# Counts as logarithms in the exponent of a gathered attention: fused add and maximum in place of mask and count products, on one Trainium2 core

## The reference, cut to what matters

```
q = (x_q @ W_q.T).reshape(b, nq, H, HD)
c_sel = c_kv[jnp.arange(b)[:, None, None], indices]
kv = (c_sel @ W_kv_up.T).reshape(b, nq, K, 2, H, HD)
scores = jnp.einsum('bqhd,bqkhd->bqkh', q, k) * SCALE
attn = jax.nn.softmax(scores, axis=2)
out = jnp.einsum('bqkh,bqkhd->bqhd', attn, v).reshape(b, nq, d)
return out @ W_out.T
```

## Time and profile before

| | us |
|---|---|
| median of 3 runs | 1254.29 (1249.91 to 1254.9) |
| the profiled execution | 1254.05 |
| its span | 1252.6 |
| PE busy | 1171.6 (94%) |
| DVE busy | 980.0 (78%) |
| ACT busy | 913.4 (73%) |
| POOL busy | 640.3 (51%) |
| granted PE clock, mean | 0.975 of full |

### The profile page before, as it was taken

How to read it: one execution, slowest core, us unless ns; L and a number is a source line. 1 busy time by engine, 2 the same in 40 slices (tenths; PEclk the granted TensorE clock), 3 DMA queues, 4 the chain that set the end, 5 groups by cost and what they waited for, 6 DMA issues and landing times.

```text
span 1252.6 us, 30881 instructions
## 1 busy us (share of the span) xinstructions
PE 1171.6 (94%) x12256; PEld 952.0 (76%) x12256; DVE 980.0 (78%) x2026; ACT 913.4 (73%) x2290; POOL 640.3 (51%) x632
## 2 busy tenths in 40 slices
PE   2668999999999999999999999999999999999986
PEld 1446878788887777888888788888887888878864
DVE  3655888888888888888888888888888888877642
ACT  2365778778777877777778778777787787777751
POOL 2413455655544655554456555544565555445553
PEclk7877999999999999999999999999999999999998
DMA  8233112222221222122212221222222212212111
GB/s 285 69 72 98 49 49 59 49 55 72 59 56 41 58 53 54 37 53 64 83 45 58 49 55 40 53 59 51 83 58 49 59 38 52 59 39 52 30 25 23
DMA packets 82246, 74.82 MB, mean 60 GB/s; under 512 B 33017, under 2 KB 66239, under 8 KB 82102
## 3 DMA queue, kind: packets, MB, share of 16 engines
q1 hardware_dynamic: 81670, 71.89, 22.6%
q10 hardware_dynamic: 432, 0.95, 0.2%
HBM read 39.98 MB, written 15.52 MB: 44 GB/s over the span
## 4 chain that ended last, share of the span: by engine, by line
PE 85%; DMA 5%; SPq 3%; ACT 3%; DVE 2%; POOL 1%; issue 1%; ACTq 0%; POOLq 0%; DVEq 0%
PE F L391 15%; PE F L737 5%; PE TA L684 5%; PE F L385 5%; PE F L789 5%; PE F L764 5%; PE F L725 5%; PE F L800 4%; PE F L655 3%; PE SA L673 3%; PE SA L678 3%; PE F L794 3%; PE MA L691 3%; PE F L960 3%; PE TA L385 2%; PE F L781 2%
## 5 line engine op out<-in xcount | busy, mean ns | idle before, releaser
L1334 POOL TENSOR_TENSOR ZREST<-HID,ZPARTS 128x128 f32<-128x128 f32 x32 | 13.8, 431 | 218.9 <-ACT ZPARTS L1205 218.9
L1365 POOL TENSOR_TENSOR LS<-LS,ZABS 128x1024 f32<-128x1024 f32 x32 | 75.5, 2359 | 58.0 <-ACT ZABS L1278 58.0
L673 PE MATMUL SA<-MASK,minus 128*128 128x308 bf16 x256 | 73.0, 298 | 22.0 <-DMA QS<-q_dram 20.7
L665 DVE TENSOR_REDUCE PACKED<-HOT 128x19 int32<-128x1216 bf16 x64 | 92.2, 1441 | 0.1
L1321 POOL CAST IW<-IDX 128x64 f32<-128x64 int32 x32 | 8.0, 250 | 160.9 <-DMA IDX<-idx_dram 160.9
L684 PE MATMUL TA<-CONST,EXPS 128*128 128x128 f32 x512 | 87.6, 294 | 0.8 <-ACT OT L1270 0.8
L1355 POOL TENSOR_TENSOR QM<-QD,ISEXPT 128x1024 f32<-128x1024 f32 x32 | 75.9, 2372 | 5.0 <-DMA QD<-QG 4.9
L684 PEld LDWEIGHTS TA<-CONST,EXPS 128*128 128x128 f32 x512 | 72.0, 209 | 6.5 <-issue 5.1
L1357 POOL TENSOR_TENSOR AT<-AT 128x1024 f32<-128x1024 f32 x32 | 75.9, 2371 | 0.8 <-DVE AT L1055 0.8
L1358 POOL TENSOR_TENSOR QM<-QD,ISEXPT 128x1024 f32<-128x1024 f32 x32 | 76.0, 2375 | 0.0
L678 PE MATMUL SA<-KNOW,QS 128*128 128x154 bf16 x512 | 73.1, 232 | 0.0
(11 more groups left out here) (269 smaller groups left out, 3958.7 us busy)
## 6 DMA issues: line engine op xcount, KB each, us to landing
QD<-QG SPq DMA_DIRECT2D x128, 128.0 KB, 2.4
QS<-q_dram SPq DMA_DIRECT2D x64, 192.0 KB, 3.2
q_dram<-QPARTS SPq DMA_DIRECT2D x32, 192.0 KB, 2.1
XA<-x_dram SPq DMA_DIRECT2D x32, 128.0 KB, 2.2
QS<-q_dram SPq DMA_DIRECT2D x32, 128.0 KB, 2.4
XB<-x_dram SPq DMA_DIRECT2D x32, 128.0 KB, 3.0
out_dram<-OUT SPq DMA_DIRECT2D x32, 128.0 KB, 1.7
KNOW<-k_dram SPq DMA_DIRECT2D x4, 616.0 KB, 4.6
```

The costliest lines, as they stand in the source:

```text
L665: return dve.tensor_reduce(PACKED[:, r], HOT[:, r, :], AX.X, ALU.add)
L673: pe.matmul(SA[:, i, 0:2 * NKV], minus[:, :], MASK[t % 2][:, :].unsqueeze(1).to_broadcast([P, 2, NKV]), start=True, stop=False, skip_group ...
```

## The change

Counts enter before the exponential, as `LNC` = ln(count + 1e-30), with -1e30 added where the count is under 0.5. ACT makes the logarithm, POOL the rest, once a tile:

```diff
-                act.activation(COUNTR[:, :, :], COUNT[:, P:NPAD].unsqueeze(2).to_broadcast([P, RPAD, GH]), ACT.Copy).then_inc(s_a_counts_act, 1)
-                act.activation(COUNTT[a % 2][:, :, :], spares, ACT.Copy).then_inc(s_a_countt, 1)
-                act.activation(MASK[a % 2][:, :], COUNT[:, 0:NKV], ACT.Relu, bias=const("masked"), scale=MASKED).then_inc(s_a_counts_act, 1)
+                act.activation(LN[:, :], COUNT[:, 0:NKV], ACT.Ln, bias=const("tiny")).then_inc(s_a_lncount, 1)
...
+                pool.tensor_scalar(OFF[:, :], COUNT[:, 0:NKV], 0.5, MASKED, ALU.is_lt, ALU.mult).then_inc(s_a_off, 1)
+                pool.tensor_tensor(LNC[a % 2][:, :], LN[:, :], OFF[:, :], ALU.add).then_inc(s_a_counts_pool, 1)
```

The mask matmuls and the count transposes go. The maximum becomes one fused instruction for each head, which writes -(s + LNC) back to PSUM and keeps its minimum; the exponential then has scale -1:

```diff
-                pe.matmul(SA[:, i, 0:2 * NKV], minus[:, :], MASK[t % 2][:, :].unsqueeze(1).to_broadcast([P, 2, NKV]),
-                          start=True, stop=False, skip_group_check=True)
...
+        def maxima(t, out):
+            for h in range(GH):
+                s = score_banks[:, h // 2, h % 2, :]
+                last = dve.tensor_tensor_reduce(s, s, LNC[t % 2][:, :], -1.0, LARGE, ALU.add, ALU.min, out[:, h:h + 1])
+            return last
...
-                dve.tensor_reduce(MAXS[:, 0, :].rearrange("p (a h) -> p a h", a=2), score_banks, AX.X, ALU.max, negate=True).then_inc(s_b_max, 1)
+                maxima(b, MAXS[:, 0, :]).then_inc(s_b_max, 1)
...
-                act.activation(EXPS[:, 0, 0:NKV, 0], score_banks[:, 0, 0, :], ACT.Exp, bias=MAXS[:, 0, 0:1])
+                act.activation(EXPS[:, 0, 0:NKV, 0], score_banks[:, 0, 0, :], ACT.Exp, bias=MAXS[:, 0, 0:1], scale=-1.0)
```

`TA` and `MA` become neighbouring banks of one tile `TM`, so that the five transposed blocks of a group are 640 columns in a row (`ROWS`) and leave PSUM in one copy: on DVE for groups 0 and 2, on ACT for groups 1 and 3:

```diff
-                dve.tensor_tensor(PR[0][:, :], MA[:, 3 * P:4 * P], COUNTT[b % 2][:, 1, :], ALU.mult).then_inc(s_b_probr, 1)
-                dve.tensor_tensor(PT[0][:, :, :], TA[:, :].rearrange("p (h q) -> p h q", h=GH), COUNTT[b % 2][:, 0, :].unsqueeze(1).to_broadcast([P, GH, P]), ALU.mult).then_inc(s_b_probs, 1)
+                dve.tensor_copy(PT[0][:, :], ROWS).then_inc(s_b_probs, 1)
...
-                dve.tensor_tensor(PT[1][:, :, :], TA[:, :].rearrange("p (h q) -> p h q", h=GH), COUNTT[b % 2][:, 0, :].unsqueeze(1).to_broadcast([P, GH, P]), ALU.mult).then_inc(s_b_probs, 1)
-                dve.tensor_tensor(PR[1][:, :], MA[:, 3 * P:4 * P], COUNTT[b % 2][:, 1, :], ALU.mult).then_inc(s_b_probr, 1)
+                act.activation(PT[1][:, :], ROWS, ACT.Copy).then_inc(s_b_probs_act, 1)
```

More of the change, by code:

```diff
@@ L152, in program @@
         XNT = sb("XNT", [P, KD, P])
-        MASK = two("MASK", [P, NKV], bf16)
-        COUNTT = two("COUNTT", [P, 2, P])
+        LN = sb("LN", [P, NKV])
+        OFF = sb("OFF", [P, NKV])
+        LNC = two("LNC", [P, NKV])
         QT = sb("QT", [P, KD, P])
@@ L162, in program @@
         EXPS = sb("EXPS", [P, 2, NPAD, GH])
-        PT = two("PT", [P, GH, P])
-        PR = two("PR", [P, P])
+        PT = two("PT", [P, (GH + 1) * P])
         OT = sb("OT", [P, GROUPS, P])
@@ L694, in values @@
                 h = g * GH + hh
-                last = pe.matmul(o[VW * hh:VW * hh + VW, :], v[:, h * VW:(h + 1) * VW], PT[g % 2][:, hh, :],
+                last = pe.matmul(o[VW * hh:VW * hh + VW, :], v[:, h * VW:(h + 1) * VW], pt[:, cols(hh)],
                                  start=False, stop=True, skip_group_check=True)
@@ L839, in pe_tiles @@
                 transposes(C0, XM[:, :], KD).then_inc(s_c_xmt_ps, 1)
-            if 0 <= b < TILES:
-                scores(b, 1).then_inc(s_b_scores, 1)
+            if 0 <= d < TILES:
+                pe.wait_ge(s_d_k1, d + 1)
+                pairs(D2, lambda k, p: WQKB[:, cols(p)], lambda k: HQ[d % 2][:, :]).then_inc(s_d_q2_ps, 1)
             if 0 <= a < TILES:
@@ L852, in pe_tiles @@
             if 0 <= d < TILES:
-                pe.wait_ge(s_d_k1, d + 1)
-                pairs(D2, lambda k, p: WQKB[:, cols(p)], lambda k: HQ[d % 2][:, :]).then_inc(s_d_q2_ps, 1)
+                pe.wait_ge(s_d_exp2, 3 * d + 3)
+                transposes(D0, flat(K2[d % 2][:, :, :]), NP).then_inc(s_d_k2t_ps, 1)
             if 0 <= c < TILES:
@@ L861, in pe_tiles @@
                 hidden(XMT[c % 2]).then_inc(s_c_hidden_ps, 1)
[L862 to L866, removed]
             if 0 <= b < TILES:
-                pe.wait_ge(s_b_probs, 4 * b + 1)
-                values(b, 0).then_inc(s_b_values, 1)
+                pe.wait_ge(s_b_probs, 2 * b + 1)
+                values(b, 0, PT[0]).then_inc(s_b_values, 1)
+                pe.wait_ge(s_b_exps2_1, b + 1)
+                scores(b, 2).then_inc(s_b_scores, 1)
             if 0 <= c < TILES:
@@ L873, in pe_tiles @@
             if 0 <= d < TILES:
[L874 to L878, removed]
+                pe.wait_ge(s_d_q2, d + 1)
+                inner(KG1T, Q1).then_inc(s_d_a1_ps, 1)
             if 0 <= c < TILES:
@@ L883, in pe_tiles @@
                 pe.wait_ge(s_b_ot, 4 * b + 1)
-                exp_transposes(1).then_inc(s_b_exps_ps, 1)
+                exp_transposes(EXPS[:, 1]).then_inc(s_b_exps_ps, 1)
+            if 0 <= d < TILES:
+                pe.wait_ge(s_d_kg2, d + 1)
+                transposes(D0, flat(KG1T[:, :, :]), NP).then_inc(s_d_k1t_ps, 1)
+                pe.wait_ge(s_d_at1, d + 1)
+                inner(KG2T, QG2).then_inc(s_d_a2_ps, 1)
+            if 0 <= b < TILES:
+                pe.wait_ge(s_b_probs_act, 2 * b + 1)
+                values(b, 1, PT[1]).then_inc(s_b_values, 1)
+            if 0 <= c < TILES:
+                pe.wait_ge(s_c_zmin, 3 * c + 1)
+                v_product(XMT[c % 2]).then_inc(s_c_v_ps, 1)
             if 0 <= d < TILES:
@@ L1046, in dve_tiles @@
-                dve.tensor_tensor(PR[1][:, :], MA[:, 3 * P:4 * P], COUNTT[b % 2][:, 1, :], ALU.mult).then_inc(s_b_probr, 1)
+                dve.wait_ge(s_b_scores, 4 * b + 4)
+                maxima(b, MAXS[:, 1, :]).then_inc(s_b_max, 1)
+                dve.wait_ge(s_b_exps_ps, 4 * b + 3)
+                dve.tensor_copy(PT[0][:, :], ROWS).then_inc(s_b_probs, 1)
+            if 0 <= c < TILES:
+                dve.wait_ge(s_c_rexp, c + 1)
+                dve.tensor_reduce(RT[:, 2:3], ELOG[:, :], AX.X, ALU.add).then_inc(s_c_router, 1)
```

399 lines of the change are left out of this document (186 added, 213 removed).

## The result

The changed kernel takes 1259.36 us (median of 9 runs, 1256.86 to 1259.87) against 1252.35 for the kernel before (9 runs). The ratio is 1.0051, with a 95% interval of 1.0039 to 1.0063: about half a per cent slower, where 1232 us and 1.8% less were forecast. The profiled spans are 1258.6 and 1252.6 us.

The account below looks back on a forecast made before the run. PE was taken to bound the kernel, with DVE arriving last at the second `inner` after the change. Period 35.2 for 35.94 saves 21 us over 29 iterations, draining 1: 1254 - 22 = 1232 us, range 1212 to 1266.

Parts of the forecast that it names:

- PE, what goes: Mask matmuls leave PE, 1.05 us an iteration; PE reaches the second `inner` at T0 + 14.91, 19.71 remain; PE-only period 34.6.
- T0: Start on PE of the scores of group 0 in an iteration; times within the iteration count from it.
- DVE, what comes: DVE gets 16 fused pairs an iteration and two copies for four pairs; net only +0.2 us an iteration.
- t: DVE slot of one fused add-and-minimum pair, body plus read: taken as 0.30 us, bounds 0.25 to 0.46.
- 11.9 + 12 t: When DVE's `AT1` lets the second `inner` start, in us after T0; 15.5 with t = 0.30.
- The new wait: PE waits 0.6 us at the second `inner` for DVE's `AT1`, part of it earlier, at the transposes of `XN`.
- the rival at 1287 us: Fused body and read each wait for the other's end: t = 0.46, period 37.1, slower; chance 0.18.
- the forecast of 35.2: Steady period in us, 15.5 to the second `inner` plus 19.7 after it; 0.72 less than 35.94.
- ACT, POOL and SP at nothing, "0 to 0.5 us an iteration": Extra ACT and POOL work and unchanged SP DMAs cost nothing, being covered; 0 to 0.5 us kept for the range.
- The filling waits for the same DMAs.: The first iterations, before the steady period, wait for the same DMAs as before; no change in time counted.
- delays one ACT copy: POOL's `QREST`, behind another product of 2.37 us, delays an ACT copy ahead of `OT`'s second copy; costed at nothing.
- rival 2: Gain eaten: t 0.34 to 0.38, or 0.5 us of ACT-POOL waits; period 35.7 to 36.2, 1246 to 1260 us; chance 0.20.

## Why the prediction was wrong

- **PE, what goes.** Right: scores 0.27, rest of the iteration 19.70. PE's own arrival at the second `inner` was put at T0 + 14.91. With the exponential moved it is 15.22, of which 0.28 is the wait for `XN`: 14.94 without. Single distances changed both ways (`L707` 1.08 us for 0.90, the transposes of `K` 0.64 for 0.53, a wait of 0.21 for `XN` in the kernel before gone) and nearly cancel; why was not tried.
- **DVE, what comes.** t was 0.30 and is 0.27; the read costs no slot. The formula for `AT1`, 11.9 + 12 t, gives T0 + 15.1 with this t; in the kernel with the exponential moved it is ready at 14.91 (268.90 + 0.06 - 254.05). The rule of the Trainium skill that the next instruction waits for an empty pipeline, and with it the rival at 1287 us, did not come true; the section itself adds that an instruction that is not held starts earlier, and the starts 0.07 to 0.08 before the end of the one ahead agree with that.
- **The new wait.** Half right. PE does wait for a later DVE, but not at `inner`, in neither kernel: the wait is at `XN`, where the prediction put a part of it, 0.28 in place of 0.6. Nor does it hang on t: `KG1T`, moved ahead of `XN`, waits there for PE. So that 34.91 came near the forecast of 35.2 is partly luck. In the changed kernel PE loses 0.90 at the gate products and 0.35 at `XN`, counted from start to start, 1.25 together: 14.94 + 1.25 = 16.19.
- **ACT, POOL and SP at nothing, "0 to 0.5 us an iteration" for the range.** This is the step that failed. The bound was made by adding up busy time and by asking who waits for a late result. An engine that is early or late by 3 us can also do harm by what it runs beside. `SG` on `K` cost 0.98 us a period; 29 of these would be 28 us, and the span with the exponential moved is 26.2 us shorter (1232.4 for 1258.6), more than the whole forecast gain of 22. To see it, one had to follow `SG`: its start at 609.32 in the iteration of the earlier trace rows, its release by ACT's exponential, and the four copies of 0.6 us that now stand ahead of that.
- **"The filling waits for the same DMAs."** Wrong by 5.2 us. In iteration 1 POOL had 7 us of work queued behind the two new instructions. In the steady state, where they were weighed, they cost nothing.
- **`QREST` "delays one ACT copy".** Right as a mechanism, and worth nothing in steady iterations; in the middle ones `QM` ahead of it waits for `QD`, PE waits 0.51 us for `OT` at 638.27, and this made up most of the 5.7 us of long periods.
- **The size against the rivals.** The time fell where rival 2 had put it (1246 to 1260), but neither of its causes holds as it stands: t was small, and though ACT's late exponential released POOL's product late, what it cost was DVE's time beside POOL, not a wait between ACT and POOL.

The Trainium skill has the rule that was missing. Its page "SBUF — State Buffer", section "Who interferes with whom", says that a DVE instruction with two SBUF inputs contends with a GpSimd instruction that reads SBUF. It also says, of DVE's two-port modes, that whoever issues first has the shared ports for its whole instruction while the other is blocked. The runs agree with both: `K` 1.78 us for 0.69, `COUNT` 2.46 for 0.47, a scalar operation 0.86 for 0.23, ending 0.55, 0.18 and 0.03 us after POOL's instruction, which began first; a reciprocal and a reduction under `SG` are as short as ever (0.20 and 0.68).

## What to carry to other kernels

When a change reorders one engine, list for DVE and POOL what each runs beside the other, before and after: an operation that starts behind the other's long one (0.04 to 0.44 us in these rows) can be lengthened to that one's end, and here this turned a relief of 1 us an iteration, some 30 us, into a loss of 45. The trace shows it as one group whose mean duration has grown to two to five times, with no bracket on it; the brackets stand on the engine that waits behind. Compare starts, not brackets, before calling an engine the only bound: 0.28 us an iteration stood here without one, behind a DVE instruction that waits for PE and had been put ahead of one that PE waits for. And work out the filling iterations by themselves, since an instruction that is free in the steady state can hold up a queue there.

## What was not expected of the hardware

- A fused operation with an accumulated result is two instructions, but the read of the accumulator (0.13 to 0.14 us) starts together with the next body and costs no slot: pairs start every 0.24 to 0.28 us.
- DVE can hold POOL as well: `QREST` takes 1.53 us in the mean under DVE's `WEIGHT` product and 0.71 in the changed kernel, where it lies elsewhere.
- With four columns only, `VALS` takes 0.76 us in the mean in the kernel after and 0.37 before; it ends 0.01 to 0.04 us after POOL's `QREST` or `QM`, whichever runs beside it. It does not stand in the chain that ended last.
- An idle time of PE of 1.36 to 1.38 us was followed by a mean granted clock of 0.72 over 6 us in 9 of 27 iterations of one kernel, and by 1.00 in the other 18 and in the kernel before; what decides was not tried.
